# Running sums in PSUM: the residual stream of a four-layer decoder stays in four accumulator banks

## The reference, cut to what matters

```
h = layernorm(x) @ Win.T + bin                          # 2048 tokens x 128
for each of 4 layers:
    y = silu(layernorm(h) * l1w + l1b)
    y = sconv(y)                                        # complex decaying running sum along the sequence
    h = h + y * scl
    y = silu((layernorm(h) * l2w + l2b) @ W1.T + b1)    # 128 -> 512
    h = h + y @ W2.T + b2                               # 512 -> 128
x = x + layernorm(h) @ Wout.T + bout
```

## Time and profile before

| | |
|---|---|
| median of 3 runs | 1124.79 us (1124.3 to 1128.26) |
| the profiled execution: its own time | 1125.29 us |
| the profiled execution: span of the core | 1123.5 us |
| mean granted TensorE clock | 0.951 |
| busy: TensorE matmul / VectorE / ScalarE / GpSimd | 1009.7 / 565.4 / 373.1 / 446.7 us |
| start of the layers (turn of visit 1, slot 0) | 96.9 us |
| last `scale` of the layers (visit 19) | 377.88 us |

### The profile page before, as it was taken

One profiled execution on the slowest core, in us unless ns is written; L12 is line 12 of the kernel. 1 busy time (PEld: TensorE's weight loads), 2 busy tenths in 40 slices (PEclk: granted clock), 3 DMA queues, 4 the chain that ended last, 5 costly groups with the idle time before them and its releaser, 6 DMA issues. The chain is left out here.

```text
span 1123.5 us, 13340 instructions
## 1 busy us (share of the span) xinstructions
PE 1009.7 (90%) x3528; PEld 533.5 (47%) x3535; DVE 565.4 (50%) x1661; ACT 373.1 (33%) x1014; POOL 446.7 (40%) x562
## 2 busy tenths in 40 slices
PE   6788889999998969799737999999999999999995
PEld 6686555555544435334423444444444444444442
DVE  5645789999986879969985111111111111111111
ACT  2433768778764338668620000000000000000000
POOL 3833456455552010009505444444344443333331
PEclk9878999999998989999868999999999999999998
DMA  7320111110000330004695373464637346373332
GB/s 301 132 75 1 48 48 39 57 39 1 1 1 1 150 132 20 1 1 169 259 381 184 75 223 76 110 192 123 183 79 230 81 131 174 77 224 75 75 75 38
DMA packets 38462, 120.25 MB, mean 107 GB/s; under 512 B 6220, under 2 KB 9351, under 8 KB 38408
## 3 DMA queue, kind: packets, MB, share of 16 engines
q1 hardware_dynamic: 25592, 79.77, 19.3%
q0 software_dynamic: 12816, 39.86, 16.3%
HBM read 82.91 MB, written 36.70 MB: 106 GB/s over the span
## 5 line engine op out<-in xcount | busy, mean ns | idle before, releaser
L2008 PE MATMUL bank<-T,X 128*128 x1184 | 508.4, 592 | 0.8 <-DVE X L2056 0.8
L2008 PEld LDWEIGHTS bank<-T,X 128*128 128x128 f32 x1184 | 224.9, 190 | 284.0 <-issue 284.0
L2070 DVE TENSOR_SCALAR X<-bank,col_p 128x512 f32<-128x512 f32 x37 | 27.8, 751 | 399.5 <-PE bank L2008 399.5
L2036 ACT ACTIVATE X<-bank,col_p 128x512 f32<-128x512 f32 x37 | 25.4, 687 | 495.1 <-PE bank L2008 495.1
L1961 POOL DMA_INDIRECT X<-x_nrm,col_s x156 | 150.6, 965 | 71.6 <-issue 46.9
L1970 POOL DMA_INDIRECT out_dram<-X,col_d x37 | 60.0, 1621 | 262.8 <-DVE X L2070 244.3
L470 POOL TENSOR_TENSOR rs<-ve,neg_half 128x4 f32<-128x4 f32 x36 | 37.4, 1040 | 116.8 <-DVE ve L951 116.8
L636 PE MATMUL bank<-nat,T 128*128 128x512 f32 x128 | 69.9, 677 | 10.5 <-issue 7.8
L817 ACT ACTIVATE M<-X,T 128x256 bf16<-128x256 f32 x152 | 74.9, 496 | 0.5 <-POOLq L466 0.5
L805 ACT ACTIVATE X<-bank,T 128x512 f32<-128x512 f32 x64 | 43.9, 687 | 58.3 <-PE bank L636 56.7
L226 POOL TENSOR_TENSOR late<-late,neg_half 128x1 f32<-128x1 f32 x32 | 17.8, 556 | 112.6 <-DVE late L222 112.6
(11 more groups left out here) (333 smaller groups left out, 1444.1 us busy)
## 6 DMA issues: line engine op xcount, KB each, us to landing
T<-in_L_ffn_expert_w_dram SPq DMA_DIRECT2D x8, 4096.0 KB, 17.5
out_dram<-X SPq DMA_DIRECT2D x17, 512.0 KB
M<-in_x_dram SPq DMA_DIRECT2D x16, 512.0 KB, 7.3
X<-in_x_dram SPq DMA_DIRECT2D x16, 512.0 KB, 6.3
x_nrm<-H SPq DMA_DIRECT2D x16, 512.0 KB, 3.5
T<-in_ctx_dram SPq DMA_DIRECT2D x9, 512.0 KB, 3.6
X<-x_nrm,col_s POOLq DMA_INDIRECT x156, 3.6
X<-in_ctx_dram SPq DMA_DIRECT2D x4, 512.0 KB, 7.0
```

The source lines that it names most:

```text
L2008: mm = nc.tensor.matmul(bank[2 * u + n][:, :], xgt[u][:, k, :], Tf[:, ds(odd * D + (k * N + n * BANK), BANK)], start=(k == 0), stop=(k == ...
```

## The change

The four chunks of the residual stream stay in PSUM through all layers, one bank for each (`HB`), and every matmul of `z` and `back` adds to it. The identity matmul that put a chunk into `OB` is done in `z` of the first four visits only. The biases b2 are not in the bank; the table column `B2` holds their running sum over the layers (a scan on VectorE in the set-up), and whoever reads the bank adds it. `middle` moves from VectorE to ScalarE, where it is a square and a copy out of the bank, as in `last`, and it stands ahead of the silus of `hidden`. Both layernorms spread into one bank (`BC`). The means of squares no longer have a bank: the first ones lie in `HD[1]`, the second ones in `HD[0]`, so `hidden` waits before its second matmul until `plus_eps(s+2)` has read. `plus_eps(s+2)` moves to the front of VectorE's slot, ahead of `turn_in(s+1)`. The small matmuls of `prepare` step 2 move into the bank `TURN`, behind the second `fill` and its reader, and their VectorE part moves to the next slot.

```diff
-        BC1, BC2, ZB, OB, HD, SMALL, TURN = 0, 1, 2, 3, (4, 5), 6, 7
+        HB, BC, HD, TURN = (0, 1, 2, 3), 6, (4, 5), 7
+        EMB, EMB_BC, EARLY_VAR = 3, 2, 1
...
+            return bank[HD[0] if not first else EARLY_VAR if v < 3 else HD[1]][:, 0:TPC]
+        def h_bank(v):
+            return bank[HB[v % CH]][:, :]
+        def bias_so_far(v, out_):
+            layer = v // CH if out_ else v // CH - 1
+            return layer_par[:, layer, B2:B2 + 1] if layer >= 0 else 0.0
...
 def var_first(v):
                     if v >= 1:
                         pe.wait_ge(ve1, v)
-                    if 3 <= v < VISITS + 3:
-                        pe.wait_ge(ve2, v - 2)
-                    if v >= 1:
-                        pe.wait_ge(b1_set, min(max(v - 2, 0) // CH, NL - 1) + 1)
+                    else:
+                        pe.wait_ge(wo_set, 4)
+                    if v == 3:
+                        pe.wait_ge(emb_tpev, 2 * NT)
+                    if v >= CH:
+                        pe.wait_ge(hid_act, (v - CH + 1) * FT)
...
 def spread_first(v):
+                    if v >= 3:
+                        pe.wait_ge(yn2, min(v - 2, VISITS))
+                    spread(v, BC, bc1)
 def var_second(v):
-                    pe.wait_ge(ve1, v + 3)
+                    if v >= 1:
+                        pe.wait_ge(hid_act, (v - 1) * FT + 3)
 def spread_second(v):
+                    pe.wait_ge(yn1, v + 3)
+                    spread(v, BC, bc2)
 def z(v):
-                    if v >= 1:
-                        pe.wait_ge(h_mid, v)
+                    if v >= CH:
+                        pe.wait_ge(h_out, v - CH + 1)
                     else:
+                        pe.wait_ge(emb_ev, v + 1)
+                        pe.wait_ge(ve1, 3 if v == 1 else 1)
                         pe.wait_ge(e_bcs, CH)
+                        nc.tensor.matmul(h_bank(v), ident[:, :], chunk(H, v), start=True, stop=True)
+                    nc.tensor.matmul(h_bank(v), cs[v // CH % 2], chunk(a_buf, v), start=False, ...)
+                    nc.tensor.matmul(h_bank(v), cs[v // CH % 2], chunk(b_buf, v), start=False, ...).then_inc(z_mm, 1)
 def hidden(v):
+                        if t == 1:
+                            pe.wait_ge(ve1, v + 4)
 def back(v, first, last):
-                        if v >= 1:
-                            pe.wait_ge(h_out, v)
                         pe.wait_ge(h_mid, v + 1)
-                        nc.tensor.matmul(bank[OB][:, :], ident[:, :], chunk(H, v), start=True, stop=False)
 def prepare(p, step):              # TensorE
                     if step == 2:
                         pe.wait_ge(w1_u, p + 1)
-                        pe.wait_ge(ve1 if p == 0 else ve2, max(CH * p, 1))
+                        turn_free()
                         for t in range(FT):
-                            mm = nc.tensor.matmul(bank[SMALL][:, 32 + t:33 + t], w1u[...], layer_par[...], start=True, stop=True)
+                            mm = nc.tensor.matmul(bank[TURN][:, t:t + 1], w1u[...], layer_par[...], start=True, stop=True)
                         mm.then_inc(b1_mm, 1)
+                        in_turn[0] = [(b1_set, p + 1)]
...
# TensorE's slot
                     if b0 is not None:
                         fill(b0, 2 * h0)
-                    for p, step in prepared(s):
-                        if p > 0 and step == 2:
-                            prepare(p, step)
...
                     if b0 is not None:
                         fill(b0, 2 * h0 + 1)
                     for p, step in prepared(s):
-                        if p == 0 or step < 2:
-                            prepare(p, step)
+                        prepare(p, step)
                     if 0 <= s + 3 < FINAL:
                         var_first(s + 3)
...
# ScalarE
+                def middle(v):
+                    act.wait_ge(z_mm, v + 1)
+                    a.activation(chunk(sq, v), h_bank(v), ACT.Square, bias=bias_so_far(v, False)).then_inc(sq2, 1)
+                    a.activation(chunk(H, v), h_bank(v), ACT.Identity, bias=bias_so_far(v, False)).then_inc(h_mid, 1)
...
+                    if 0 <= s < VISITS:
+                        middle(s)
                     if 0 <= s - 1 < VISITS:
                         hidden(s - 1)
-                    if 0 <= s < VISITS:
-                        act.wait_ge(h_mid, s + 1)
-                        square(s, sq2)
...
# VectorE's slot
+                    if 0 <= s + 2 < FINAL:
+                        plus_eps(s + 2, True, var1, ve1)
                     if 0 <= s + 1 < VISITS:
                         turn_in(s + 1)
                     for p, step in prepared(s - 1):
-                        if p > 0 and step == 0:
+                        if p > 0 and step in (0, 2):
                             prepare(p, step)
                     if b7 is not None:
                         without_under(b7, h7)
-                    if 0 <= s < VISITS:
-                        middle(s)
-                    if 0 <= s + 2 < FINAL:
-                        plus_eps(s + 2, True, var1, ve1)
...
-                link(v_.tensor_copy(layer_par[:, :, B2], bank[1][:, 0:NL]))
+                link(v_.tensor_tensor_scan(layer_par[:, :, B2], ones[:, 0:NL], bank[1][:, 0:NL], 0.0, ALU.mult, ALU.add))
```

More of the change, by code:

```diff
@@ L336, in var_at @@
         def var_at(v, first):
-            at = (0 if first else 2 * TPC) + (v % 2) * TPC
-            return bank[SMALL][:, at:at + TPC]
+            return bank[HD[0] if not first else EARLY_VAR if v < 3 else HD[1]][:, 0:TPC]
[4 more added lines that the diff above has]
+            return layer_par[:, layer, B2:B2 + 1] if layer >= 0 else 0.0
         def tile_y(b, i):
@@ L640, in back @@
                         pe.wait_ge(w2_set, v // CH + 1)
[L641 to L642 removed]
                         pe.wait_ge(h_mid, v + 1)
[L644 removed]
                     for t in range(first, last):
                         pe.wait_ge(hid_act, v * FT + t + 1)
[L647 removed]
+                        mm = nc.tensor.matmul(h_bank(v), w2c[v // CH % 2][:, t, :], hid[:, v % 2, t, :], start=False, stop=(t == FT - 1), skip_group_check=True)
                     if last == FT:
@@ L679, in prepare @@
                         pe.wait_ge(w1_u, p + 1)
-                        pe.wait_ge(ve1 if p == 0 else ve2, max(CH * p, 1))
+                        turn_free()
                         for t in range(FT):
-                            mm = nc.tensor.matmul(bank[SMALL][:, 32 + t:33 + t], w1u[:, t * P:(t + 1) * P], layer_par[:, p, LN2B:LN2B + 1], start=True, stop=True)
+                            mm = nc.tensor.matmul(bank[TURN][:, t:t + 1], w1u[:, t * P:(t + 1) * P], layer_par[:, p, LN2B:LN2B + 1], start=True, stop=True)
                         mm.then_inc(b1_mm, 1)
+                        in_turn[0] = [(b1_set, p + 1)]
                 def x_turned(t):
@@ L700, in embedded @@
                     for k in range(KD):
-                        mm = nc.tensor.matmul(bank[OB][:, u * P:(u + 1) * P], win_t[:, k, :], x_t[t % 2][:, k, :], start=(k == 0), stop=(k == KD - 1))
+                        mm = nc.tensor.matmul(bank[EMB][:, u * P:(u + 1) * P], win_t[:, k, :], x_t[t % 2][:, k, :], start=(k == 0), stop=(k == KD - 1))
                     mm.then_inc(emb_mm, 1)
@@ L854, in x_copies @@
                     act.wait_ge(e_bc, q + 1)
-                    a.copy(chunk(sq, q), bank[ZB][:, :]).then_inc(e_bcs, 1)
+                    a.copy(chunk(sq, q), bank[EMB_BC][:, :]).then_inc(e_bcs, 1)
                 act.wait_ge(set_pe, 3)
@@ L943, in turn_out @@
                     v_.tensor_tensor(by_seq(a_buf, v), by_seq(a_buf, v), cos_t[:, v // CH:v // CH + 1, :].to_broadcast([P, BPC, S]), ALU.mult).then_inc(a_back, 1)
-                def middle(v):
-                    dve.wait_ge(z_mm, v + 1)
-                    v_.tensor_tensor(chunk(H, v), chunk(H, v), bank[ZB][:, :], ALU.add).then_inc(h_mid, 1)
                 def plus_eps(v, first, var_done, done):
@@ L951, in plus_eps, with scale @@
                     v_.tensor_scalar(ve[:, v % CH, :], var_at(v, first), EPS, None, ALU.add).then_inc(done, 1)
-                def scale(v, src, bc_done, done):
-                    if v >= CH:
-                        hold(dve, h_out, v - CH + 1)
+                def scale(v, ready, n, bc_done, done):
+                    if n > 0:
+                        hold(dve, ready, n)
                     dve.wait_ge(bc_done, v + 1)
-                    v_.tensor_tensor(chunk(yn, v), chunk(H, v), bank[src][:, :], ALU.mult).then_inc(done, 1)
+                    v_.tensor_tensor(chunk(yn, v), chunk(H, v), bank[BC][:, :], ALU.mult).then_inc(done, 1)
                 def stats(b, h):
@@ L1050, in prepare @@
                         dve.wait_ge(b1_mm, p + 1)
-                        v_.tensor_tensor(b1f[p % 2], bank[SMALL][:, 32:32 + FT], layer_par[:, p, B1:B1 + FT], ALU.add).then_inc(b1_set, 1)
```

(7 more changed lines are left out.)

22 lines of the change are left out of this document (9 added, 13 removed).

## The result

The changed kernel takes 1129.93 us (median of 15 runs), the kernel before 1125.19 us beside it: ratio 1.0034, 95% interval 1.0026 to 1.0043, without one run of each: 1158.57 us of the changed kernel, in a slower state with a mean granted clock of 0.900, and 3684.2 us of the kernel before. Its profiled execution takes 1129.04 us, span 1127.2 us, against 1125.29 and 1123.5 us: 3.7 us longer. The mean granted TensorE clock is 0.943, before 0.951.

What follows compares the result with a forecast made beforehand. VectorE was taken to set the time in slots 4 to 12. Slot, start and end terms summed to +0.9 us, plus 2 for the clock, about +3: 1127.5 us on the median of 1124.79, range 1116 to 1135.

Steps and rivals of the forecast that it cites:

- the clock: TensorE idle 1.8 us in one piece before prepare in odd slots lowers its clock: 0 to 7 us, taken as 2.
- the tail: From slot 12's statistics to the last scale, the missing identity and waits removed save 4.4 us.
- the start: Set-up and slots 0 to 2: slot 3's statistics come 1.6 us later, 0.5 from set-up and 1.1 from slots 0 to 2.
- the stall at the front: VectorE's plus_eps waits 3.0 us for var_first behind prepare and the second copy; slots 3, 7, 11 each 2.4 us longer.
- Rival 1: The front stall does not come and the change pays as meant: -9 us, 1116 us; chance 0.18.
- Slots 5 and 9: No change: the saved add vanishes in a wait for step 0's transposes that was there before.
- Slots 6 and 10: var_first is ready in time, so the saved add counts whole: 0.6 us shorter each.
- the reserve of 0.5 us: With step 1 behind the second copy, the variance is ready 16.2 us into the slot, needed at 16.7.
- Slots 4 and 8: Saved add plus the vanished stall for the second variance: 1.3 us shorter in slot 4, 1.0 in slot 8.
- rival 2: Half clock falls into every odd slot, 7 us on top of +0.9: +8 us, 1133 us; chance 0.32.
- The idle before the silus: ScalarE's idle time before the silus of hidden, covering the moved middle, was to fall by about 1 us a slot.
- Rival 3: The middle on ScalarE is late and delays work behind it: +4 us more, 1131 us; shares the likeliest case's chance, 0.50.

Runs made afterwards that it cites:

- e3: Changed kernel with four extra filler matmuls in TensorE's hole ahead of prepare in slots 3, 5, 7, 9 and 11: 1130.19 us.
- e1: Changed kernel with var_first put ahead of prepare in TensorE's slot, from slot 1 on: 1119.41 us.
- e2: Changed kernel with step 2 of prepare in columns of its own, at its former places on TensorE and VectorE: 1122.11 us.
- e4: Kernel before the change with only plus_eps(s+2) moved to the front of VectorE's slot, ahead of turn_in: 1128.76 us.
- e6: e1 with two filler matmuls ahead of the second fill and two behind var_first in slots 3, 5, 7, 9 and 11: 1119.42 us.
- e7: Changed kernel with middle(s) on ScalarE behind hidden(s-1) instead of ahead of it: 1143.2 us.
- e9: Changed kernel with 0.60 us of VectorE given back per slot by doing turn_in twice, where the middle add stood: 1142.85 us.
- e10: Changed kernel with 0.86 us of TensorE given back per visit by a matmul of zeros where the identity stood: 1139.88 us.
- e8: Changed kernel with plus_eps(s+2) put back behind turn_in, prepare and without_under on VectorE: 1132.99 us.
- e5: Changed kernel with the changes of e1 and e2 together: 1120.09 us.

## Why the prediction came out right, point by point

**The forecast of 1127.5 us was 2.4 us below the median, on the right side of before, and within its own range** (forecast +2.7 us on before, measured +4.7). That the total fits so well is in part luck. At the last `scale` 2.9 us were forecast, 2 of them for the clock, and 3.13 measured, but slots 3 to 11 came 3.4 us and the tail 1.4 us dearer than in the table's forecast, and the start 2.6 us cheaper. The main step, the stall at the front, was right in place and size: slots 3 and 7 got 2.45 and 2.55 us longer (2.4), slot 11 too once the half clock is filled (e3: 16.77 - 14.24 = 2.5). e1 and e2 show the cause from two sides: free the variance of the second copy and the stall of slot 8 falls from 2.83 to 0.82 and 0.76 us. e4 shows that the place on VectorE alone costs 1 us in such slots. Rival 1, that the stall would not come, is out.

**Slots 5 and 9** were to stay: -0.09 and +0.40. L1043 (now L1055) waits no longer, as forecast. But VectorE stands 0.55 us for the second variance of slot 9 (259.55), where I had expected no such wait; TensorE had been at half clock from 251.5 to 255 us. e1 confirms what was held up there: with the variance first they fall by 1.4 and 1.9 us.

**Slots 6 and 10** were to gain 0.6 and gained nothing. The failed step is the reserve of 0.5 us that I worked out behind step 1: `plus_eps` stood 0.57 and 0.40 us at the front of slots 7 and 11. With step 1 behind the variance (e1) both slots take 15.84 us, just 0.6 below before.

**Slots 4 and 8** gained 0.98 and 1.25 (forecast 1.3 and 1.0). **The tail** gave 3.0 of 4.4 us.

**The start** was 2.6 us too dear: slot 3's statistics came 0.97 us earlier, not 1.6 later. At slot 0 they were still 1.64 us late. In slots 0 to 2 2.6 us came back, 1.3 of it in slot 1, where the kernel before has a stretch of 3.4 us at half clock from 118 on and the changed one none. e1 has the same start and 6.8 us of it: slot 1 takes 22.18 instead of 19.76 us; e6, with the same instructions as e1 up to there, has none and takes 19.36. So this term holds a piece of 3 us that my trace of the slots could not give, and that differs between runs of the same instructions.

**The clock.** It fell as forecast (half clock 47.8 for 30.7 us), and what my sum without it leaves over in slots 3 to 11 is 3.4 us where I took 2. Of these, 1.3 belong to slots 6 and 10, whose miss has the cause just named, and 1.5 to slot 11, where e3 shows the clock. But the hole was not 1.8 us in one piece: the second `fill` itself waited for the first copy, so it was 0.47 and 1.06 us. And the price does not stand as a price of the whole: e3 took 13.7 us of half clock out of the layers and was 2.9 us earlier at the last `scale`, but 6.8 us of half clock came back behind the layers and all but 0.7 us of the lead with it. In e6 against e1 10.2 us went and 13.6 came back. No run supports rival 2's 7 us. The Trainium skill (TensorE: Matmul & The Clock Gate, "A second HAM failure mode: psum-queue depth-cycling") says of another kernel that small holes between groups of matmuls make the clock swing, and that this costs throughput. The swings are in these traces; what they cost over a whole run no pair of runs here separates.

**ScalarE.** The middle costs 0.57 us from start to start for each of its two operations, ahead of `hidden`, and delays nothing that a row shows. The idle before the silus did not fall by 1 us a slot: 44.7 us against 43.8. The slots grew longer and so did the wait. Rival 3, that the middle is late, was only tested from its other side (e7).

**What the saved work was worth.** Given back one by one, the add costs 12.9 us and the identity 10.0 by the medians, where I had priced 6 and 4 to 5. But the stretch for which I had priced them, from the statistics of slot 3 to the last `scale`, grew by 7.7 us in e9 and by 4.9 in e10, not far from the price. The rest of the profiled runs' 17.2 and 11.1 us lies ahead of slot 3 (6.7 and 4.2 us, of the latter 3.5 in slot 1 with its half clock) and behind the layers (2.9 and 2.0 us). So the price of the work in the layers was nearly right; what the saved work is worth over a whole run, without the clock that came with it, no run here separates. Taken at their medians, and if the two add up, which no run here shows, the rest of the change costs not some 14 us (6 + 5 + 2.9) but about 28 (12.9 + 10.0 + 4.7), clock included. Of that, e1 gives 10.5 back by one move. The remainder, in the shared bank (7.6 us of waits once `plus_eps` leaves the front, e8) and the front place (e4), was not taken apart further.

**The faster version.** The changed kernel with `var_first` ahead of `prepare` (e1) beats both: 1119.41 us, 0.5% below before. e5 and e6 add to it nothing that can be told apart.

## What to carry to other kernels

When a reader moves to the front of one engine's list, look up what stands ahead of its writer on the other engine: here two microseconds of stall came from small matmuls that nobody needed yet and that themselves waited for a copy, queued before the ones that VectorE stood for. The same reordering was worth nothing before the change, so a list has to be put in order again after every change of who waits for whom. Price saved work by giving it back in the new kernel, one piece at a time, and read the price stretch by stretch; pieces off the path of the old kernel may be on that of the new one. And before a gain is put down to an edit, look where it arises in the trace: e6's lead over e1 lay ahead of its first filler.

## What the runs showed of the hardware that was not expected

The same hole on TensorE, 3.53 us, was followed by full clock in the changed kernel and by half clock in e1; TensorE in slot 1, first the changed kernel, then e1, then e6, which has the same instructions as e1 up to slot 3:

```profile
120.15 1.98 PE L654 MATMUL bank<-nat,T 128*128 128x512 f32 x4 [3.53 <-ACT X L823]
```

```profile
121.01 3.78 PE L654 MATMUL bank<-nat,T 128*128 128x512 f32 x4 [3.53 <-ACT X L827]
```

```profile
120.02 1.98 PE L654 MATMUL bank<-nat,T 128*128 128x512 f32 x4 [3.53 <-ACT X L835]
```

Windows of e1 there:

```profile
117.60:121.00 3.40, 0.00 (x0) 0.00 (x0) 2.97 (x6) 3.40 (x12) 1.24 (x4) 0.79 0.16 25
121.00:124.40 3.40, 3.39 (x4) 1.51 (x5) 0.00 (x0) 1.22 (x2) 2.73 (x7) 0.50 0.91 293
```

The length of a hole alone does not tell the clock behind it, and neither do the hole and the instructions around it together: between e1 and e6 the same ones went either way. What decides it, these traces do not show. And ScalarE reads a PSUM bank in 0.586 us without a bias from a table and in 0.680 with one (L805, 128x512, 4 and 11 instructions, both forms above).
